# Cross attention on one core: the next queries product ahead of the values product

## What is computed

```python
q = (query @ Wq + bq).reshape(b, sq, N_HEAD, KEY_DIM)
k = (key @ Wk + bk).reshape(b, key.shape[1], N_HEAD, KEY_DIM)
v = (value @ Wv + bv).reshape(b, value.shape[1], N_HEAD, VALUE_DIM)
scores = jnp.einsum('bqhd,bkhd->bhqk', q, k) / TEMP
attn = jax.nn.softmax(scores, axis=-1)
out = jnp.einsum('bhqk,bkhd->bqhd', attn, v).reshape(b, sq, N_HEAD * VALUE_DIM)
out = out @ Wo + bo + residual
```

## Time and profile before

| what | value |
|---|---|
| time, median of 3 runs | 2184.95 us (2184.82 to 2186.15) |
| profiled execution: time, span | 2187.32 us, 2185.6 us |
| PE busy | 2117.3 us, 97% of the span |
| PEld busy | 1855.5 us, 85% |
| DVE busy | 1609.6 us, 74% |
| ACT busy | 1280.6 us, 59% |
| POOL busy | 675.7 us, 31% |

### The profile page before, as it was taken

The page is one execution under the profiler, slowest core; times in us unless marked ns, Lnnn a source line. Parts: engine busy times, 40 slices in busy tenths (PEclk is TensorE's granted clock), DMA queues, the critical chain, the costliest instruction groups (busy, mean ns, idle before and its releaser), DMA issues.

```text
span 2185.6 us, 46111 instructions
## 1 busy us (share of the span) xinstructions
PE 2117.3 (97%) x15864; PEld 1855.5 (85%) x15865; DVE 1609.6 (74%) x3025; ACT 1280.6 (59%) x3067; POOL 675.7 (31%) x620
## 2 busy tenths in 40 slices
PE   8999999999999999999999999899998999999997
PEld 7898888888888888888888888677776888888886
DVE  6667768778777677687687786699996767666665
ACT  5556566556566565566565665477775335555553
POOL 4011011011010010110110101188885234777775
PEclk9999999999999999999999999999999999999999
DMA  4001010010010010010100100244433222333332
GB/s 153 10 21 34 0 34 24 10 34 19 14 34 19 15 34 14 19 32 2 34 24 10 34 10 1 63 153 153 151 121 100 87 78 51 54 55 53 53 55 42
DMA packets 100685, 103.90 MB, mean 48 GB/s; under 512 B 11952, under 2 KB 90160, under 8 KB 100624
## 3 DMA queue, kind: packets, MB, share of 16 engines
q1 hardware_dynamic: 86992, 84.47, 12.4%
q0 software_dynamic: 13632, 18.62, 5.2%
HBM read 72.52 MB, written 30.54 MB: 47 GB/s over the span
## 4 chain that ended last, share of the span: by engine, by line
PE 56%; DVE 17%; issue 10%; POOL 10%; ACT 4%; DMA 2%; DVEq 1%; POOLq 0%; SPq 0%; ACTq 0%
PE banks L906 29%; PE banks L949 5%; PE banks L991 5%; PE banks L1001 5%; POOL out_dram L2378 4%; PE banks L976 4%; POOL r_x L2342 3%; PE banks L2217 3%; DVE q_st L652 2%; POOL index L2349 2%; DVE s_peak L1535 2%; DVE s_rsum L1581 2%; ACT probs L541 2%; DVE z L846 1%; DMA out_dram<-r_y,index 1%
## 5 line engine op out<-in xcount | busy, mean ns | idle before, releaser
L906 PE MATMUL banks<-ctxT_hi,qk_hi 128*128 128x256 f32 x1024 | 300.5, 293 | 0.0
L906 PE MATMUL banks<-ctxT_hi,qk_lo 128*128 128x256 f32 x1024 | 289.5, 283 | 0.0
L906 PE MATMUL banks<-ctxT_lo,qk_hi 128*128 128x256 f32 x1024 | 288.4, 282 | 0.0
L541 ACT ACTIVATE probs<-banks,nbias 128x256 f32<-128x256 f32 x512 | 236.6, 485 | 71.6 <-DVE nbias L674 71.2
L548 ACT ACTIVATE pc<-banks 128x512 f32<-128x512 f32 x256 | 153.0, 598 | 191.3 <-PE banks L906 186.5
L632 DVE TENSOR_TENSOR qk_lo<-banks,qk_hi 128x512 fp32r<-128x512 f32 x256 | 165.8, 685 | 68.9 <-ACT qk_hi L503 68.8
L906 PE MATMUL banks<-pT_hi,ctx_hi 128*128 128x512 f32 x512 | 206.2, 403 | 4.7 <-DVE qk_lo L632 3.1
L432 POOL TENSOR_TENSOR rstd<-mv,power 128x2 f32<-128x2 f32 x32 | 22.2, 694 | 597.0 <-DVE mv L724 597.0
L632 DVE TENSOR_TENSOR pT_lo<-banks,pT_hi 128x512 fp32r<-128x512 f32 x256 | 164.6, 684 | 56.3 <-ACT pT_hi L503 55.7
L906 PE MATMUL banks<-pT_hi,ctx_lo 128*128 128x512 f32 x512 | 201.6, 394 | 0.0
L906 PE MATMUL banks<-pT_lo,ctx_hi 128*128 128x512 f32 x512 | 200.2, 391 | 0.0
(11 more groups left out here) (271 smaller groups left out, 6062.4 us busy)
## 6 DMA issues: line engine op xcount, KB each, us to landing
ctx_raw<-in_ctx_dram SPq DMA_DIRECT2D x64, 256.0 KB, 2.7
experts_w<-in_L_ffn_We_dram SPq DMA_DIRECT2D x24, 512.0 KB, 4.0
x_in<-in_x_dram SPq DMA_DIRECT2D x16, 256.0 KB, 2.8
x_again<-in_x_dram SPq DMA_DIRECT2D x16, 256.0 KB, 2.9
x_stream<-z SPq DMA_DIRECT2D x16, 256.0 KB, 2.2
s_x<-x_stream SPq DMA_DIRECT2D x32, 128.0 KB, 3.7
s_x_again<-x_stream SPq DMA_DIRECT2D x32, 128.0 KB, 2.1
x_normalised<-s_xl SPq DMA_DIRECT2D x32, 128.0 KB, 1.7
```

Source lines behind the costliest of these rows:

```text
L541: nc.scalar.activation(probs[:, s % 2, p, :], scores[:, s % 2, p // 2, (p % 2) * SK:(p % 2 + 1) * SK], ACT.Exp, bias=nbias[:, s % 2, p:p + ...
L906: last = nc.tensor.matmul(out, a, b, start=(n == 0), stop=(n == 3 * len(pairs) - 1))
```

## The change

In steps 2 and 6 the queries product comes ahead of the values product: in the order of the ring, on TensorE, and on the two engines that empty the banks. On ScalarE the copy into oT moves behind the exponentials and q_st, on VectorE behind q_st. No instruction is added or left out.

```diff
@@ ring_order
+        if b == 2 and (g.next if half else g.cur):
+            out += [("q", half, m) for m in range(2)]
         if b == 2 and (g.cur if half else g.prev):
             out += [("v", half, j) for j in range(2)]
-        if b == 2 and (g.next if half else g.cur):
-            out += [("q", half, m) for m in range(2)]
@@ scalar
                 if s == 6 and g.next:
                     xT_upper(g)
+                if g.cur and s in (2, 3, 6):
+                    exps(g, s)
...
+                if b == 2 and (g.next if half else g.cur):
+                    for m in range(2):
+                        q_upper(g, half, m)
                 if b == 2 and (g.cur if half else g.prev):
 
                     bank, free = wait_filled(act, g, ("v", half, 0))
...
                     last.then_inc(free, 1)
-                if g.cur and s in (2, 3, 6):
-                    exps(g, s)
...
-                if b == 2 and (g.next if half else g.cur):
-                    for m in range(2):
-                        q_upper(g, half, m)
@@ vector
                 if s == 6 and g.next:
                     xT_lower(g)
-                if b == 2 and (g.cur if half else g.prev):
-                    bank, free = wait_filled(dve, g, ("v", half, 1))
...
-                    last.then_inc(free, 1)
...
                 if b == 2 and (g.next if half else g.cur):
                     for m in range(2):
                         q_lower(g, half, m)
+                if b == 2 and (g.cur if half else g.prev):
+                    bank, free = wait_filled(dve, g, ("v", half, 1))
...
+                    last.then_inc(free, 1)
@@ tensor
                     do_ctxT(g, b)
                 if s == 6 and g.next:
                     do_xT(g)
+                if b == 2 and (g.next if half else g.cur):
+                    do_q(g, half)
                 if b == 2 and (g.cur if half else g.prev):
                     do_v(g, half)
-                if b == 2 and (g.next if half else g.cur):
-                    do_q(g, half)
```

More of the change, by code:

```diff
@@ L593, in scalar @@
                         q_upper(g, half, m)
+                if b == 2 and (g.cur if half else g.prev):
+                    bank, free = wait_filled(act, g, ("v", half, 0))
+                    for i in range(2):
+                        pair = (1 - half) * PAIRS + i
+                        last = nc.scalar.activation(oT[:, pair, :], bank[:, i * GT:(i + 1) * GT], ACT.Identity,
+                                                    bias=bv[:, pair:pair + 1])
+                    last.then_inc(free, 1)
                 if b == 3:
@@ L843, in vector @@
                         q_lower(g, half, m)
+                if b == 2 and (g.cur if half else g.prev):
+                    bank, free = wait_filled(dve, g, ("v", half, 1))
+                    for i in range(2):
+                        pair = (1 - half) * PAIRS + 2 + i
+                        last = nc.vector.tensor_scalar(oT[:, pair, :], bank[:, i * GT:(i + 1) * GT],
+                                                       bv[:, pair:pair + 1], None, ALU.add)
+                    last.then_inc(free, 1)
                 if s == 6 and g.prev:
```

## The result

The changed kernel takes 2246.07 us (median of 4 runs, 2245.26 to 2247.8) against 2184.89 of the kernel before (4 runs): a ratio of 1.0277, 95% interval 1.0264 to 1.029, or 61 us more. The forecast was 2254 us, with 2226 to 2268 as its range.

The account below looks back on a forecast made before the run. The prediction took TensorE's in-order stream to bound the loop. Step 6 wait 46, less 3 and 6 coming back, plus step 2 wait 15 and clock 17, made 69 us more: 2254 us, range 2226 to 2268.

Parts of the forecast that it names:

- What bounds the loop: Cross attention loop: TensorE's in-order stream is the path, busy 1202.82 of 1210.00 us; its waits add nearly one for one.
- The wait in step 6: Step 6, groups 0 to 14: TensorE idles until VectorE ends xT_lo, 15 x 3.07 = 46 us; lower bound 1.9 each.
- What comes back: Behind the stall, waits for q_st (step 6) and ctxT_lo (step 7) go: 3 us and 6 us less.
- The wait in step 2: Step 2, groups 1 to 15: the context product waits for the queries' banks, 1.0 us each, 15 us; bounds 0 and 1.3.
- The clock: After the step 6 stalls the granted clock falls: 12 of 15 times, 1.4 us each, 17 us; bounds 0 and 26.
- the sign that I had set: In the loop, a granted clock under 1.00 in most of the 15 places of the step 6 stall.
- The sum: Whole kernel: 46 - 3 - 6 + 15 + 17 = 69 us more, a median of 2254 us.
- that the clock stays up: Rival, step 6 stalls: no fall of the clock follows them; 2237 us, chance 0.22 for 2228 to 2240.
- absorbed stalls: Rival: step 2 costs nothing, step 6's stall is 1.9 us; 2200, or 2217 with clock falls; chance 0.11.
- A gain or no change: Two rivals, whole kernel: faster, at most 10 us, 2175 (chance 0.02); or time unchanged (chance 0.02).

Follow-up runs that it names:

- run with xT_lo first: The changed kernel, with VectorE in step 6 making ctxT_lo and xT_lo ahead of the scores' maximum instead of behind it: 2213.98 us, ratio 1.013.
- step 2 alone: The kernel before, with the queries product ahead of the values product in step 2 only: 2202.37 us against 2186.0, ratio 1.0076.
- the filled wait: The changed kernel, with TensorE transposing the identity 26 times while it waits for xT_lo in step 6: 2234.26 us, ratio 1.0221.
- step 6 alone: The kernel before, with the queries product ahead of the values product in step 6 only: 2237.51 us, ratio 1.0236.
- the later split: The kernel before, with GpSimd splitting a group's first context block behind step 7's first context product instead of step 6's: 2182.3 us, ratio 0.9985.
- all three edits: The kernel before with queries first in step 2 and q_st ahead of the exponentials, bo added later, and GpSimd's split later: 2168.78 us, ratio 0.9925.

## Why the prediction was right

- **What bounds the loop**: right. Wherever a wait of TensorE was added or taken away, the time moved with it, though not always by its length: a new wait gives the other engines time to catch up (45.3 us of waits cost 32.5), and a repaired one can bring up the next (7.8 us of a weight load's waits gone, 8.5 come).
- **The wait in step 6**: forecast 15 x 3.07 = 46 us, measured 45.3 over 15 waits, 3.07 from start to start in group 5. That VectorE would not come earlier held too: the maximum starts 1.15 us behind the scaling, as before. The run with xT_lo first shows that its place in the queue makes the wait, and gives 1.57 us in place of it.
- **What comes back**: sized too small. I took 0.17 + 0.4 us a group; 3.07 - 2.17 = 0.9 came back. The waits for q_st and for ctxT_lo that I named are gone, but in step 7 I priced one gap of 0.32 us with some small change, at 0.3 to 0.7, and 1.06 came back there (8.04 us from the first to the last fold, then 6.98). That fold not only started 0.32 us late: the context product behind it came another 0.32 late, and what follows up to the last fold 0.42 more. The 1.06 and 0.15 for q_st, less some 0.2 by which the queries and the context product take longer in their new places (3.05 for 2.95, 2.88 for 2.74), make about the 0.9 measured. One further reason that VectorE is early now, the z instructions at less than half their time, I had not seen; how much of the 1.06 it gives no run separates.
- **The wait in step 2**: forecast 1.0 us a group, by 0.74 and 0.42 (its own times give 0.71 and 0.39) less 0.17; measured 0.84 and some 0.3, and 1.09 in all by step 2 alone. The cause, the exponentials ahead of q_st on ScalarE, is shown by turning them round.
- **The clock**: the size was nearly right for a reason that was partly wrong. I took 12 falls of 1.4 us, 17 in all. There were 6 groups with 9 spells of 3.4 us, and 12.9 us by the filled wait, 1.43 for a spell. Per spell the estimate held; the number of groups did not, nor did the sign that I had set, a clock under 1.00 in most of the 15 places, and no row of the kernel before could give it. So it is partly luck that this term came out within 4 us: the same wait in step 6 alone brought 14 falls and 19.0 us. The rule of the Trainium skill ("TensorE: Matmul & The Clock Gate", HAM oscillation), by which every tile behind such a wait starts cold, did not hold for all 15 waits: 9 groups kept the full clock after the same 3.0 us. In step 6 alone 14 of 15 agree with it.
- **The sum**: 45.3 + 16.4 - 12.8 + 12.9, with 12.8 for what comes back (45.3 - 32.5), gives 61.8, against the 61.2 measured and the 69 forecast. Since 12.8 and 12.9 are themselves differences of whole times, the agreement says only that the parts add. Of the 7.2 us between 69 and 61.8, 4.1 are the clock, 3.8 what came back and 0.7 the wait, less 1.4 that step 2 cost beyond the forecast.
- **The rivals**: that the clock stays up (2237) is what the filled wait gives, 2234. Of the absorbed stalls only what comes back in step 7 is true, at 1.06 us a group; the wait stayed at 3.0 and step 2 cost its 1.1. A gain or no change had no part in it.

## What to carry to other kernels

When two products change places on the engine that bounds the kernel, ask of each what its input is waiting for: a product whose input was made just before needs the other one as a cover, and here that cover was 3.6 us of unrelated work over a chain of 3.0. An edit that brings a result forward needs the queue that empties it turned as well: here step 2 alone cost 16 us as it was written and gained 6 with the exponentials behind q_st, part of it ahead of the loop. And after each repair read which wait ends last now, since the next one may stand right behind it.

## What the runs showed of the hardware

**The length of a wait alone doesn't decide whether the clock falls.** Waits of 3.0 us were followed by half clock in 6 of 15 groups of the changed kernel (twice 3.4 us in a row, or once) and in 14 of 15 of step 6 alone. Waits of 1.57 us, in the run with xT_lo first, never were. But in the run with the later split the clock was at half for 3.4 us from 195 on, and no wait of TensorE near it is longer than this one, of 0.98 us:

```profile
192.33 0.38 PE L949 MATMUL banks<-q_st,wk_hi 128*128 128x256 f32 x1 [0.98 <-DVE qk_lo L632]
```

```profile
195.00:200.00 5.00, 5.00 (x32) 5.00 (x31) 2.94 (x6) 4.33 (x12) 0.00 (x0) 0.66 0.09 33
```

From 192.93 to 194.29 TensorE had also done twelve matmuls of only 16 columns. With all three edits the same wait was followed by no fall. What decides it, the place in time or the work before, no run here separates. A wait filled with transposes of an identity kept the clock up and saved 12.9 us (both steps) and 19.0 (step 6 alone) though TensorE did nothing useful in it.

**GpSimd's split holds up VectorE.** At the outset I wrote that the engines meet only at semaphores; here one slows another, and no semaphore stands between them. z from line 846 in the kernel before, and in the changed one (page of the instruction by its line; shortest, median, longest in ns):

```profile
L846 DVE SCALAR_TENSOR_TENSOR z<-z,mv,gamma x32: 473/810/1521, 183.7 to 1412.2; 128x256 f32<-128x256 f32 x32
```

```profile
L846 DVE SCALAR_TENSOR_TENSOR z<-z,mv,gamma x32: 473/477/1482, 185.8 to 1470.3; 128x256 f32<-128x256 f32 x32
```

In the kernel before the two of group 5 run from 525.41 to 527.66 (0.81 and 1.51 us), and GpSimd splits the context then:

```profile
525.33 0.62 POOL L416 CAST ctx_hi<-ctx_raw 128x512 fp32r<-128x512 f32 x1 [19.28 <-PE banks L906]
526.03 1.35 POOL L418 TENSOR_TENSOR ctx_lo<-ctx_raw,ctx_hi 128x512 fp32r<-128x512 f32 x1
```

In the changed kernel the split starts behind them, at 546.60, and they take 0.87 us together. With the later split on the kernel before they are at 0.48 each too, but now a small instruction of the maximum, which is 0.16 us elsewhere, takes 0.89 (its row, at 532.34, is shown with that run), beside this on GpSimd:

```profile
531.91 1.30 POOL L418 TENSOR_TENSOR ctx_lo<-ctx_raw,ctx_hi 128x512 fp32r<-128x512 f32 x1
```

The fold's subtractions (one input from PSUM), which run from 533.36 beside GpSimd's split of the next block (533.47 to 535.45), keep their 0.68 us each. This is what the Trainium skill says ("SBUF — State Buffer", Who interferes with whom): a VectorE instruction with two inputs in SBUF contends with a GpSimd instruction that reads SBUF, one with at most one such input, outside VectorE's two-port modes, does not. The rows agree with both halves. That the split itself is what slows z is shown by moving it; how much it would pay to move it to a place with no such instruction of VectorE beside it was not tried.
